# Joining the split layer norms of a gated linear recurrence, moving their phases, and deepening two weight streams

## The reference, cut to what matters

```
x  = x + layernorm(attn(layernorm(x)))        # half 1: gated linear recurrence
x  = x + layernorm(ffn(layernorm(x)))         # half 2: 8 experts and a shared one, unchanged

attn:  gate, xh = split(x @ W_in.T)                       # 1536 + 1536 features
       xh    = causal_conv4(xh)
       f, i  = split(xh @ W_gates.T)
       alpha = exp(-8 * softplus(forget_base) * sigmoid(f))
       beta  = sqrt(1 - alpha**2 + 1e-6)
       h_t   = alpha_t * h_(t-1) + beta_t * sigmoid(i)_t * xh_t
       out   = (gelu(gate) * h) @ W_out.T
```

## Time and profile before

| | |
|---|---|
| timed runs | 5685.91 and 5942.24 us, median 5814.07 us |
| the profiled execution | 5589.6 us |
| its span, slowest core (core 3) | 5588.1 us |
| spans of the 8 cores | 5570.0 to 5588.1 us |
| busy: PE, DVE, ACT, POOL | 74%, 42%, 22%, 11% of the span |

### The profile page before, as it was taken

How to read it: one execution, slowest core, us unless ns; L and a number is a source line. 1 busy time by engine, 2 the same in 40 slices (tenths; PEclk the granted TensorE clock), 3 DMA queues, 4 the chain that set the end, 5 groups by cost and what they waited for, 6 DMA issues and landing times.

```text
span 5588.1 us, 52370 instructions; the slowest of 8 cores (5570.0 to 5588.1 us)
## 1 busy us (share of the span) xinstructions
PE 4129.6 (74%) x16496; PEld 1627.0 (29%) x16496; DVE 2358.0 (42%) x3808; ACT 1229.3 (22%) x1779; POOL 629.1 (11%) x1187
## 2 busy tenths in 40 slices
PE   4566566666474656688889888887588898888885
PEld 1222222222121221233333333331233333333331
DVE  2423422413323153544554444544444554444544
ACT  1332331314032231111221111121111221111221
POOL 1010011110111101011111111110011111111110
PEclk8788788888787877799999999998799999999997
DMA  4444444534343332133334333332134343334341
GB/s 61 65 72 64 62 75 64 83 51 72 57 64 57 58 57 34 31 61 65 62 61 76 55 63 66 62 58 55 23 61 68 52 75 63 61 62 67 53 74 40
DMA packets 179707, 336.66 MB, mean 60 GB/s; under 512 B 19456, under 2 KB 39952, under 8 KB 179312
## 3 DMA queue, kind: packets, MB, share of 16 engines
q0 software_dynamic: 175280, 324.92, 36.6%
q1 hardware_dynamic: 4160, 8.39, 0.4%
HBM read 649.41 MB, written 8.39 MB: 118 GB/s over the span
## 4 chain that ended last, share of the span: by engine, by line
PE 64%; DVE 12%; DMA 9%; ACT 9%; issue 5%; DVEq 0%; POOL 0%; ACTq 0%; POOLq 0%
PE pb L165 64%; ACT bufA L938 4%; DMA wi<-wi_xh 3%; DMA wg<-wgates 3%; DMA wo<-wout 2%; DMA wi<-wi_gate 1%; DVE sa L554 1%; DVE sa L539 1%; ACT L534 1%; ACT ssf L534 1%; DVE ssf L409 1%; DVE sxnbf L415 1%; ACT L588 1%; DVE ssi L548 1%; DVE ssi L551 1%
## 5 line engine op out<-in xcount | busy, mean ns | idle before, releaser
L165 PE MATMUL pb<-xn,wq 128*128 128x512 bf16 x9216 | 2040.1, 379 | 267.0 <-ACT bufA L938 267.0
L165 PEld LDWEIGHTS pb<-xn,wq 128*128 128x128 bf16 x9216 | 882.0, 98 | 1430.5 <-issue 412.1
L165 PE MATMUL pb<-sxh,wg 128*128 128x512 bf16 x2304 | 645.8, 448 | 289.9 <-DMA wg<-wgates 170.0
L165 PE MATMUL pb<-a_s,w2s 128*128 128x512 bf16 x2304 | 551.9, 403 | 123.8 <-DVE a_s L993 123.8
L938 ACT ACTIVATE bufA<-pb,c_b1g 128x512 f32<-128x512 f32 x256 | 175.9, 687 | 1680.5 <-PE pb L165 1680.5
L165 PE MATMUL pb<-sxnbf,wi 128*128 128x512 bf16 x1152 | 327.1, 428 | 237.8 <-DMA wi<-wi_xh 111.3
L943 DVE SCALAR_TENSOR_TENSOR bufA<-pb,c_b3g,bufA 128x512 f32<-128x512 f32 x256 | 192.2, 751 | 674.7 <-ACT bufA L938 674.7
L165 PEld LDWEIGHTS pb<-sxh,wg 128*128 128x128 bf16 x2304 | 250.2, 112 | 685.2 <-issue 515.7
L165 PEld LDWEIGHTS pb<-a_s,w2s 128*128 128x128 bf16 x2304 | 232.7, 103 | 434.7 <-issue 200.6
L972 DVE TENSOR_TENSOR bufA<-bufA,bufC 128x512 f32<-128x512 f32 x288 | 199.5, 693 | 241.0 <-ACT bufC L967 241.0
L967 ACT ACTIVATE bufC<-bufA 128x512 f32<-128x512 f32 x288 | 181.3, 629 | 467.5 <-DVE bufA L962 467.4
(11 more groups left out here) (147 smaller groups left out, 2897.2 us busy)
## 6 DMA issues: line engine op xcount, KB each, us to landing
wg<-wgates POOLq DMA_DIRECT2D x192, 384.0 KB, 4.7
wq<-w1g POOLq DMA_DIRECT2D x128, 256.0 KB, 5.0
wq<-w3g POOLq DMA_DIRECT2D x128, 256.0 KB, 6.8
wq<-w1l POOLq DMA_DIRECT2D x128, 256.0 KB, 7.6
wq<-w3l POOLq DMA_DIRECT2D x128, 256.0 KB, 8.4
w2s<-w POOLq DMA_DIRECT2D x128, 256.0 KB, 5.1
wi<-wi_xh POOLq DMA_DIRECT2D x96, 256.0 KB, 3.8
wi<-wi_gate POOLq DMA_DIRECT2D x48, 256.0 KB, 3.8
```

The source lines that it names most:

```text
L165: t.matmul(o, l, r, start=s1, stop=s2),
```

## The change

It does five things. The statistics, rows and spreading of a norm become one function (`lngate`), emitted in one piece. The load of the next x and its squares move to the front of the loop body. The first norm of the next tile, up to the spreading, moves ahead of the W_out stage; its 16 DVE operations stay behind. The second norm is finished in the same tile, behind its sums, and not in the next. `wg` gets three buffers and `wo` four, with four loads ahead. And the square root gets one ACT operation more per chunk: 1 + y by an Identity with bias 1.0, then Ln with bias 1e-6.

```diff
-            wg = WStream([asb(f"wg{j}", [128, NC_H, 128], BF16) for j in range(2)], "wg", "wg")
-            wo = WStream([asb(f"wo{j}", [128, 4, 128], BF16) for j in range(3)], "wo", "wo")
+            wg = WStream([asb(f"wg{j}", [128, NC_H, 128], BF16) for j in range(3)], "wg", "wg")
+            wo = WStream([asb(f"wo{j}", [128, 4, 128], BF16) for j in range(4)], "wo", "wo")
...
                         for mj in (mi - 1, mi):
                             a_op(lambda a, ppj=mj % 2: a.activation(
+                                    out=sa2[:, ppj, :], in_=sa2[:, ppj, :],
+                                    func=AF.Identity,
+                                    bias=np.float32(1.0), scale=1.0),
+                                 waits=[("v", yv[mj])], tag=f"y1{st}")
+                        for mj in (mi - 1, mi):
+                            a_op(lambda a, ppj=mj % 2: a.activation(
                                     out=sa2[:, ppj, :], in_=sa2[:, ppj, :], func=AF.Ln,
-                                    bias=np.float32(1.0 + 1e-6), scale=1.0),
-                                 waits=[("v", yv[mj])], tag=f"lny{st}")
+                                    bias=np.float32(1e-6), scale=1.0),
+                                 tag=f"lny{st}")
...
             for st in range(_nst):
                 main = st >= 4
-                if st - 1 >= 4:
-                    ph_ln1_rows(st - 1)
+                if st + 1 < _nst:
+                    ph_xload(st + 1)
                 if main:
                     ph_gate(st)
                 ph_wgates_mid(st)
-                if st - 1 >= 4:
-                    ph_ln1_bcast_x1(st - 1)
                 if st + 1 < _nst:
-                    ph_xload(st + 1)
+                    ph_ln0_stats(st + 1)
                 if main:
                     ph_wout(st)
                 if st + 1 < _nst:
-                    ph_ln0_stats(st + 1)
                     ph_ln0_tail(st + 1)
                     ph_front(st + 1)
                 if main:
-                    ph_ln1_stats(st)
-            ph_ln1_rows(_nst - 1)
-            ph_ln1_bcast_x1(_nst - 1)
+                    ph_ln1_x1(st)
```

More of the change, by code:

```diff
@@ L247, in build_nc, with lngate @@
         g_dma(c_sb2[:], d_sb2, tag="c")
-        def lngate_stats(srcs, sqs, tag, src_waits=None, sq_waits=None,
-                         banks=(4, 5, 6, 7), fp32=False, sq_gen=None):
+        def lngate(srcs, sqs, ten_after, tag, src_waits=None, sq_waits=None,
+                   banks=(4, 5, 6, 7), fp32=False, sq_gen=None):
             sb0, sb1, bb0, bb1 = banks
@@ L253, in lngate_stats @@
             n = len(srcs) if srcs is not None else len(sqs)
[L254 to L259, removed]
+            if srcs is not None:
+                for c in range(n):
+                    w = (list(src_waits[c]) if src_waits
+                         else ([ten_after] if c == 0 else []))
+                    t_mm(pb[sb0][0:1, :], onesv[:], srcs[c],
+                         start=(c == 0), stop=(c == n - 1),
+                         waits=(bank_wait(sb0) if c == 0 else []) + w,
+                         tag=f"{tag}sx")
             if sq_gen is not None:
@@ L262, in lngate_stats @@
                 for c in range(n):
-                    gw = [("t", rel[c - 2])] if (c - 2) in rel else []
-                    ap = sq_gen(c, gw)
+                    gw = [("t", rel[c - 2])] if (c - 2) in rel else (
+                        list(sq_waits[c]) if sq_waits else [])
+                    ap = sq_gen(c, gw + (list(sq_waits[c]) if sq_waits and c >= 2 else []))
                     aw = [("a", S.n["a"])]
@@ L277, in lngate_stats @@
                          tag=f"{tag}sq")
[L278 to L285, removed]
+            tcnt = S.n["t"]
+            inv = 1.0 / (128 * n)
+            v_op(lambda v: v.tensor_scalar(out=row_m[:], in0=pb[sb0][0:1, :],
                                            scalar1=inv, scalar2=None, op0=OP.mult),
-                 waits=[("t", tcnt)] + (row_wait or []) + rg, tag=f"{tag}m")
-            v_op(lambda v: v.tensor_scalar(out=r_q[:], in0=pb[sb1][0:1, :],
+                 waits=[("t", tcnt)], tag=f"{tag}m")
+            v_op(lambda v: v.tensor_scalar(out=row_q[:], in0=pb[sb1][0:1, :],
                                            scalar1=inv, scalar2=None, op0=OP.mult),
@@ L292, in lngate_rows @@
             bank_guard[sb1] = ("v", S.n["v"])
-            v_op(lambda v: v.tensor_tensor(out=r_mr[:], in0=r_m[:],
-                                           in1=r_m[:], op=OP.mult),
+            v_op(lambda v: v.tensor_tensor(out=row_mr[:], in0=row_m[:],
+                                           in1=row_m[:], op=OP.mult),
                  tag=f"{tag}m2")
-            v_op(lambda v: v.scalar_tensor_tensor(out=r_q[:], in0=r_q[:],
-                                                  scalar=1e-5, in1=r_mr[:],
+            v_op(lambda v: v.scalar_tensor_tensor(out=row_q[:], in0=row_q[:],
+                                                  scalar=1e-5, in1=row_mr[:],
                                                   op0=OP.add, op1=OP.subtract),
@@ L300, in lngate_rows @@
             vcnt = S.n["v"]
-            a_op(lambda a: a.activation(out=r_r[:], in_=r_q[:], func=AF.Ln),
+            a_op(lambda a: a.activation(out=row_r[:], in_=row_q[:], func=AF.Ln),
                  waits=[("v", vcnt)], tag=f"{tag}ln")
-            a_op(lambda a: a.activation(out=r_r[:], in_=r_r[:], func=AF.Exp,
+            a_op(lambda a: a.activation(out=row_r[:], in_=row_r[:], func=AF.Exp,
                                         scale=-0.5), tag=f"{tag}ex")
             acnt = S.n["a"]
-            v_op(lambda v: v.tensor_tensor(out=r_mr[:], in0=r_m[:],
-                                           in1=r_r[:], op=OP.mult),
+            v_op(lambda v: v.tensor_tensor(out=row_mr[:], in0=row_m[:],
+                                           in1=row_r[:], op=OP.mult),
                  waits=[("a", acnt)], tag=f"{tag}mr")
[L309 to L314, removed]
+            vcnt = S.n["v"]
+            t_mm(pb[bb0][:, :], c_ones1[:], row_r[:], start=True, stop=True,
                  waits=bank_wait(bb0) + [("v", vcnt)], tag=f"{tag}bcr")
-            t_mm(pb[bb1][:, :], c_ones1[:], r_mr[:], start=True, stop=True,
+            t_mm(pb[bb1][:, :], c_ones1[:], row_mr[:], start=True, stop=True,
                  waits=bank_wait(bb1), tag=f"{tag}bcmr")
             return S.n["t"]
[L320 to L333, removed]
         with ExitStack() as attn_ctx:
@@ L392, in ph_ln0_stats @@
                 xw = [(pre[st]["xsem"], pre[st]["xld"]), ("c", wc)]
-                stt_ = lngate_stats([sxbf[:, c, :] for c in range(NC_D)],
+                stats_done = lngate([sxbf[:, c, :] for c in range(NC_D)],
                                     [ssqbf[:, c, :] for c in range(NC_D)],
-                                    f"ln0_{st}",
+                                    None, f"ln0_{st}",
                                     src_waits=[xw] + [[]] * (NC_D - 1),
                                     sq_waits=pre[st]["sq_v"])
-                st_state[st] = {"ln0_st": stt_}
+                st_state[st] = {"ln0_stats": stats_done}
             def ph_ln0_tail(st):
@@ L402, in ph_ln0_tail @@
                 sxbf = sxbf2[:, par]
-                stats_done = lngate_bcast(st_state[st]["ln0_st"], f"ln0_{st}")
+                stats_done = st_state[st]["ln0_stats"]
                 T0 = st * ST
@@ L537, in midchain @@
                     al_done = ("a", S.n["a"])
-                    sg2 = [guard["sa2_sq"]] if (mi < 2 and "sa2_sq" in guard) else []
                     v_op(lambda v, pp=pp: v.scalar_tensor_tensor(
@@ L541, in midchain @@
                             in1=ssf[:, pp, :], op0=OP.mult, op1=OP.mult),
-                         waits=[al_done] + sg2, tag=f"na2{st}")
+                         waits=[al_done], tag=f"na2{st}")
                     return S.n["v"]
@@ L617, in ph_wout @@
                 for pss in range(2):
-                    lis = {kk: wo.load(d_wo2[pss * NC_H + kk]) for kk in range(3)}
+                    lis = {kk: wo.load(d_wo2[pss * NC_H + kk]) for kk in range(4)}
                     for k in range(NC_H):
@@ L628, in ph_wout @@
                         wo.done(lis[k])
-                        if k + 3 < NC_H:
-                            lis[k + 3] = wo.load(d_wo2[pss * NC_H + k + 3])
+                        if k + 4 < NC_H:
+                            lis[k + 4] = wo.load(d_wo2[pss * NC_H + k + 4])
                     for mm4 in range(4):
@@ L641, in ph_wout, with ph_ln1_x1 @@
                 st_state[st]["evao_a"] = ("a", S.n["a"])
-            def ph_ln1_stats(st):
+            def ph_ln1_x1(st):
+                par = st % 2
+                T0 = st * ST
                 evao_a = st_state[st]["evao_a"]
                 sqg_g = [guard["sa2_sq"]] if "sa2_sq" in guard else []
-                mg = [g for g in (guard.get(("mid", 0)), guard.get(("mid", 1))) if g]
```

(7 more changed lines are left out.)

## The result

The changed kernel takes 0.9945 times what the kernel before takes, with a 95% interval of 0.9931 to 0.996: a gain of about half a per cent. Its median is 5568.70 us over 11 timed runs, beside 5754.65 us for the kernel before over 10 runs of the same session. The two times behind the ratio are some 5567 and 5598 us, 31 us apart.

A forecast was written before the change was run, and what follows sets the result against it. The prediction took the ACT and DVE chain plus the odd chunk's own 6.9 us to bound the W_gates loop. Its terms, 25.6 + 0 - 18 - 18 - 73 + 91 - 38 = -30 on 5589.6, gave 5560 us, range 5505 to 5630.

The forecast's parts named there:

- (a): W_gates pair in main tiles: Identity lengthens chain by 1.44 us, pair becomes 22.7 us; +6.4 per tile, +25.6 for four.
- (b): Prefix tiles: W_gates stage +2.2 us, the norm behind it -3.7; taken as 0 for the four, -8 to +16.
- (c): From T, the end of a tile's W_gates products, to W_out, tiles 4 to 6: 26.1 us each, -18 altogether.
- (d): W_out stage with four weight buffers: 35 us in place of 40.9, -18 us for three tiles.
- (e): W_out's end to third wi group: 6.3 us left of 30.5, normalising beside W_out; -73 us for three tiles.
- (f): Start of the gate: 40.7 us each in tiles 5 and 6, waits moved from W_out, 9.4 in tile 7; +91.
- (g): Tile 7, end of W_gates products to end of W_out: 37 us in place of 75.1; -38 us.
- the footing: Basis of the total: 5560 us on the profiled execution's 5589.6; the same 30 us makes 5784 beside median 5814.07.
- Weights bind: Rival in W_gates: all 170.0 us of waits for wg would go, giving 5412 us; chance 0.08.
- The slow clock takes the whole odd chunk: Rival in W_gates: after 9.6 us idle the odd chunk takes 10.5 us, not 7.7; +112, 5672 us; chance 0.12.
- The load of x delays the weights: Rival ahead of first wg or gate weights, tiles 0 to 4: 10.3 us paid five times, 5611 us; chance 0.08.

The follow-up runs named there:

- the fastest version: The changed kernel without its Identity, with the load of the next x issued inside the W_gates stage and its squares later there; 0.975 to the kernel before.

## Why the prediction was right, and where it was wrong

The forecast was -30 us on an execution of 5589.6; the runs give -31 on 5598. Its steps, with measured sizes from core 7 where nothing else is said:

- **(a) the pair**: forecast 22.7 us and +6.4 per main tile; measured 22.7 and, on the mean of cores 4 to 7, +6.8 (124.0 against 117.2). The working was right: the chain grew by the length of the two operations, the odd chunk took 7.6 us where 7.7 was put, and the third buffer removes the wait for weights without shortening the pair.
- **(b) the prefix**: +2.2 forecast for the stage, +3.3 measured; the norm behind it -3.7 forecast and -3.2 measured (21.1 us from 437.38 to the spreading at 458.49, 24.3 before). The net of 0 held. What did not hold is that weights bind the prefix pair, whose chain alone would make it 19.7: with the third buffer alone the pair takes 20.4.
- **(c) T to W_out**: 26.1 forecast, 26.0 measured.
- **(d) W_out**: 35 forecast; 36.1, 33.9 and 32.5 measured in tiles 4 to 6, -20 where -18 stood. The buffers alone gave 34.4, 33.6 and 33.3 (mean of cores 4 to 7), so this gain is theirs.
- **(e) behind W_out**: 6.3 forecast, 7.8 measured: -68 where -73 stood.
- **(f) the gate's start**: 40.7 forecast for tiles 5 and 6, 40.5 measured in tile 5. The wait moved from W_out to the gate, as forecast. The load of x alone was longer than its 10.3 us, which was the shortest of the 8 cores' medians: on core 7 the median is 13.3 before and 15.2 after. The sum did not suffer, because it took the whole stretch from the last x1 sum to the first product (10.8 us; now 1264.29 to 1276.48, 12.2), not the load's own duration.
- **(g) tile 7**: 37 forecast, 33.7 measured: -41 where -38 stood.

On the mean of cores 4 to 7 these seven terms measure +27.4, -0.5, -15.6, -20.8, -68.7, +89.0 and -40.5, together -30. But the whole first half gained 21 us on these cores, not 30. The other 9 lie mostly in stretches that the sum put at nothing without a reason: the four gate stages are 5.7 us longer together, and the front of tile 4 takes 51.1 us where it took 46.9. The second half, which the change does not touch, is 8 us shorter (3432 against 3441). On these cores it takes 3438 to 3441 us in the three profiled kernels with the old order and 3432 to 3438 in the five with the new; no run shows why. So the terms that were worked out held to a few us each, and that the total meets -31 is in part luck: +9 and -8 that the forecast did not have cancel. (The ends of its range add up to 5500 and 5621, where it wrote about 5505 and 5630; nothing rests on the difference.)

**The step that failed is the footing.** The prediction put 5560 us beside a printed median of 5814.07 and said that the same 30 us would be 5784 there. Read against that median, 5560 is a gain of 4.4%, clear of noise; what was measured is 0.55%. The median came from two runs, 5685.91 and 5942.24; among the runs of the result and of each later session the kernel before has its lowest, four or more of them, at 5591 to 5604 us, within 0.3% of the profiled execution. So the profiled execution was the right basis for the time and the median was no basis for a gain. I gave both numbers and should have said that only the difference of 30 us was forecast, some 0.5%, and that its sign rested on terms of +117 and -147 that nearly cancel.

**The rivals.** Weights bind: by that the buffers alone would have saved 148 us; they saved 55, and the pair did not shorten. The slow clock takes the whole odd chunk: behind 9.9 us of idle the odd chunk that ends a stage took 8.20 us in tile 4, 6.67 in tile 5 and 6.86 in tile 7, not 10.5; behind more than 9 us it took 6.6 to 8.3 in all main tiles of cores 4, 5 and 7, 7.4 on the mean. The Trainium skill (TensorE: Matmul & The Clock Gate, HAM oscillation) describes a loop that starts slow after each wait for data and loses only that start; the trace now agrees for waits up to 9.9 us, where it had shown 5.8. The load of x delays the weights: this happened, at the gate of tiles 5 and 6, where term (f) had it, and hardly ahead of the first W_gates groups (the longest wait for wg is 1.7 us on core 7 and 3.6 on core 5). It does happen there as soon as the load is moved behind the gate, at 13.15 us.

## What to carry to other kernels

A wait that goes from a view has gone nowhere until the row behind it is read: here 264 us of waits for weights disappeared and 31 us were gained, 89 without the Identity, because most of the same idle time lay behind a chain on other engines. When a transfer waits for a buffer in a list that issues in order, moving it moves the wait to whatever stands behind it; put it where the consumers behind it have idle time already, as inside the W_gates pairs. And a forecast that is a difference should be judged on the basis it was worked out from, after a look whether the printed median is such a basis.

## What the runs showed that was not expected

- The length of idle time hardly set what the products behind it cost: 24 products took 6.67 to 8.20 us behind 9.9 us of idle, and 6.82 to 8.29 behind 3.4 to 5.8.
- The load of x takes quite different times from issue to landing. A core's median is 10.3 to 13.5 us in the kernel before, 13.3 to 16.6 in the changed kernel (cores 4 to 7) and 12.4 to 18.1 in the fastest version. What made it longer was not measured. It still cost less inside W_gates, in the fastest version, than in the other places, since most of it lay there in time in which TensorE waited for the sigmoid anyway.
